# Cross attention and expert layer on one core: a new order of the attention matmuls, full-size output projection, a column scalar for spreading k, and an unrolled last loop

## The chip, the core and the metric

The kernel runs on one core of a Trainium2 chip. The metric is the time of one execution in microseconds (us), lower is better; the median of several executions is given. The core has a matrix engine (PE, TensorE), a vector engine (DVE), an activation engine (ACT), a general-purpose engine (POOL) and a queue engine that issues transfers (SP). Each engine works through its own list of instructions in order and waits on semaphores for the others.

## What is computed

128 batches of 64 tokens, 128 features, 16 heads of 8 features; float32 throughout, with causal masking and a mixture of experts after it (8 experts, two of them for each batch).

```python
x = x + xattn(layernorm(x), ctx, ctx, Wq, Wk, Wv, Wo)
x = x + ffn(layernorm(x), W1, b1, W2, b2, Wr, br, gamma, beta)
# xattn: q, k, v in 16 heads of 8
scores = einsum('bhqd,bhkd->bhqk', q, k) * 8 ** -0.5       # masked where key > query
out = einsum('bhqk,bhkd->bhqd', softmax(scores), v) @ Wo.T
# ffn: one routing decision for each batch, from the mean of its tokens
rw = softmax(x.mean(axis=1) @ Wr + br)                     # top 2 of 8, softmaxed again
h = gelu(x @ W1[e] + b1[e]); expert_out = h @ W2[e] + b2[e]
y = sum of the two weighted expert_out + x
out = (y - mean) / sqrt(var + 1e-5) * gamma + beta
```

## The kernel before

**Attention** (about 20 to 365 us) works on one batch in a *step*. Four steps make a *pair* P (its four batches share two tiles of 128 tokens and one load of the context); two pairs make one round of the loop in `steps(i)`. A step is called by its place in the pair, s0, s1, s2 or s3; a unit U is one batch. Every engine has its own `steps` with the same count, so the order within an engine is written out by hand.

- PE, in each step: two matmuls that put the causal mask into a score bank (L346, bfloat16, 128x128 array), four score matmuls on small tiles of the array (`scores`, L350, 32 rows by 64 columns), four transposes of the softmax of three steps before (`turn`, L361, whole array), four matmuls of it with v (`attend`, L374, 128 rows by 32 columns), for the unit of four steps before. Then, by step: s0 transposes and projects the next pair (L322, L323: `prep_xk`) and does an output projection (`project`, L387, tiles of 128 by 64); s1 transposes the second layer norm's result (L397) and computes q (L327, `prep_q`); s2 does an output projection (L387); s3 computes v (L334).
- Every float32 matmul that is no transpose leaves two records in the trace, so that four score matmuls are "x8".
- DVE: maximum of the scores (L769), sum of the previous unit's exponentials (L772), scores less their maximum (`scores_shifted`, L779), the reciprocal of the sum (L785), and the statistics of both layer norms.
- ACT: the exponential (`probs`, L586), the copy of the transposed softmax out of PSUM (`probsT`, L595), and by step: s0 four copies of v (L535) ahead of the exponential, then the second layer norm (L568); s1 the copy of x-transposed and k (L545), then attnT (L606) and z (L574); s2 the copy of q (L551); s3 the first layer norm (L559) and attnT.
- POOL: multiplies the exponentials by the reciprocals (L1064), and spreads k (L1032, `spread_k`): for each batch a copy of k for each of four heads, zero outside the head's rows, by a product of two broadcast tensors, two of them in s1 and two in s2. It also computes the reciprocal standard deviations (L1010 to L1015), and in s3 splits z into a high part (a cast, L1043) and the rest (L1045).

The score banks are two, used in turn; mask and scores of a unit wait until DVE has shifted the unit two before (`v_sub`). `turn` waits for POOL's product (`g_norm`), q for the copy of x-transposed (`a_xk`), the scores of s0 for the spread k (`g_km`).

**Routing** (about 365 to 391 us) is a chain of small operations on DVE with a few matmuls between: top two experts, the count of each, a list of slots in blocks of eight batches (`SLOTS` entries, 328), at least one block an expert.

**Expert layers** (about 391 to 590 us): 36 blocks in loops whose bounds are read at run time, each with split high and low products of both layers.

**The last stage** (about 595 us to the end) normalizes 16 groups of four tiles: PE centres (L523), ACT squares and takes the square root (L697, L701) in a run-time loop of four rounds of four groups, DVE takes the reciprocal (L941), scales (L945) and adds x to two of the four tiles (L953), POOL adds x to the other two (L1141), SP sends 256 KB to memory.

## Time and profile before

| | |
|---|---|
| median of 3 executions | 637.44 us (635.75 to 637.48) |
| the profiled execution | 637.03 us, its span 635.2 us |
| PE busy, share of the span | 578.2 us, 91% |
| DVE busy | 526.4 us, 83% |
| ACT busy | 498.8 us, 79% |
| POOL busy | 459.6 us, 72% |
| score matmuls, transposes, matmuls with v | 1024, 512 and 1024 records |

The profile is of one execution. A row of a timeline gives the start, the length, the engine, the line, what is written from what, and in brackets the idle time ahead with the engine whose work ended it. Matmuls overlap in the array, so their starts, and not their lengths, tell how fast they follow each other.

### The profile page before, as it was taken

The numbers are of one execution on the slowest core, as the hardware profiler recorded it, in microseconds if no ns is written. First come the engines' busy times: TensorE is split into PE (matmuls) and PEld (weight loads), VectorE is DVE, ScalarE is ACT, GpSimd is POOL, SyncE is SP. The second block draws the span as 40 slices with busy tenths as digits, with TensorE's granted clock in tenths as the row PEclk, the third lists the DMA queues.
The fourth block names the chain that finished last, engine by engine and source line by source line (L and its number), as shares of the span: only waits on it lengthen the run. The fifth ranks groups of instructions, "written<-read, shape, count | busy, mean of one in ns | idle before, by whom it ended". The sixth has DMA issues, their size and how long they took to land.

```text
span 635.2 us, 19482 instructions
## 1 busy us (share of the span) xinstructions
PE 578.2 (91%) x4737; PEld 380.8 (60%) x4737; DVE 526.4 (83%) x1473; ACT 498.8 (79%) x1131; POOL 459.6 (72%) x815
## 2 busy tenths in 40 slices
PE   4899999999999999999999726999999999999762
PEld 2455555555555555555555414787888788887652
DVE  3889898988989898989898756888888888897576
ACT  3587888888887878787888627888888898887595
POOL 5788999999999999999989654656655555564233
PEclk9999999999999999999999958999999999999787
DMA  3010100010010101010020011122312332322034
GB/s 101 27 35 11 35 25 23 18 33 25 10 32 25 33 8 33 25 33 8 17 74 2 2 34 53 52 80 79 95 58 61 89 92 61 93 62 63 21 118 147
DMA packets 55583, 30.03 MB, mean 47 GB/s; under 512 B 4856, under 2 KB 54528, under 8 KB 55552
## 3 DMA queue, kind: packets, MB, share of 16 engines
q1 hardware_dynamic: 55120, 29.47, 15.8%
q8 instruction: 13, 0.21, 0.1%
q10 hardware_dynamic: 432, 0.20, 0.1%
q14 instruction: 18, 0.15, 0.1%
HBM read 13.00 MB, written 4.19 MB: 27 GB/s over the span
## 4 chain that ended last, share of the span: by engine, by line
PE 83%; ACT 6%; issue 4%; DVE 3%; POOL 2%; ACTq 1%; DVEq 1%; DMA 0%; POOLq 0%
PE scores_banks L350 12%; PE bank_pair L361 12%; PE bank_pair L374 7%; PE bank L387 6%; PE scores_banks L346 6%; PE scores_banks L479 5%; PE scores_banks L480 5%; PE scores_banks L481 5%; PE bank_pair L492 5%; PE bank_pair L493 5%; PE bank_pair L494 5%; PE bank L334 3%; PE bank L323 2%; ACT squares L697 2%; PE bank L327 2%
## 5 line engine op out<-in xcount | busy, mean ns | idle before, releaser
L1064 POOL TENSOR_TENSOR probs<-probs,row_sum_recip 128x512 f32<-128x512 f32 x128 | 133.6, 1044 | 19.7 <-DVE row_sum_recip L785 17.7
L586 ACT ACTIVATE probs<-scores_shifted 128x512 f32<-128x512 f32 x128 | 80.8, 632 | 52.1 <-DVE scores_shifted L779 50.7
L676 ACT ACTIVATE gelu<-scores_banks,b_expert 128x512 f32<-128x512 f32 x144 | 98.6, 691 | 26.6 <-PE scores_banks L481 19.7
L1113 POOL CAST gathered<-z_hi_lo (+1 forms) x114 | 45.9, 438 | 88.8 <-PE scores_banks L481 79.2
L769 DVE TENSOR_REDUCE row_max<-scores_banks 128x8 f32<-128x512 f32 x128 | 87.5, 684 | 24.3 <-PE scores_banks L350 24.1
L772 DVE TENSOR_REDUCE row_sum<-probs 128x8 f32<-128x512 f32 x128 | 87.1, 680 | 17.2 <-ACT probs L586 17.1
L895 DVE SCALAR_TENSOR_TENSOR zT_then_yT<-bank_pair,slot_weight,zT_then_yT x288 | 74.8, 283 | 17.2 <-issue 15.8
L595 ACT ACTIVATE probsT<-bank_pair 128x512 f32<-128x512 f32 x128 | 76.2, 595 | 14.5 <-PE bank_pair L361 13.5
L779 DVE TENSOR_TENSOR scores_shifted<-scores_banks,row_max 128x512 f32<-128x512 f32 x128 | 86.9, 679 | 0.0
L361 PE MATMUL bank_pair<-ident,probs 128*128 128x128 f32 x512 | 83.9, 286 | 2.0 <-POOL probs L1064 1.6
L350 PE MATMUL scores_banks<-k_by_head,qT 32*64 32x256 f32 x1024 | 85.5, 403 | 0.0
L361 PEld LDWEIGHTS bank_pair<-ident,probs 128*128 128x128 f32 x512 | 53.6, 140 | 51.0 <-issue 41.2
L1032 POOL TENSOR_TENSOR k_by_head<-xnT_and_kT,mask_j 128x256 f32<-128x256 f32 x128 | 75.9, 614 | 4.8 <-ACT xnT_and_kT L545 4.8
L886 DVE TENSOR_TENSOR gelu_lo<-gelu,gelu_hi 128x512 fp32r<-128x512 f32 x108 | 71.3, 697 | 5.4 <-ACT gelu_hi L680 2.5
L680 ACT ACTIVATE gelu_hi<-scores_banks,b_expert 128x512 fp32r<-128x512 f32 x108 | 74.6, 691 | 0.0
L479 PE MATMUL scores_banks<-gathered,w_hi 128*128 (+1 forms) x144 | 56.5, 393 | 3.0 <-ACTq L665 1.7
L492 PE MATMUL bank_pair<-gelu_hi,w_hi 128*128 128x512 f32 x144 | 56.5, 392 | 1.2 <-DVE gelu_lo L886 1.1
L481 PE MATMUL scores_banks<-gathered,w_hi 128*128 (+1 forms) x144 | 56.1, 389 | 0.0
L494 PE MATMUL bank_pair<-gelu_lo,w_hi 128*128 128x512 f32 x144 | 56.1, 389 | 0.0
L493 PE MATMUL bank_pair<-gelu_hi,w_lo 128*128 128x512 f32 x144 | 56.1, 389 | 0.0
L480 PE MATMUL scores_banks<-gathered,w_lo 128*128 (+1 forms) x144 | 56.0, 389 | 0.0
L374 PE MATMUL bank_pair<-probsT,v_blocks 128*32 128x128 f32 x1024 | 54.5, 285 | 0.0
(169 smaller groups left out, 1168.7 us busy)
## 6 DMA issues: line engine op xcount, KB each, us to landing
gathered<-z_hi_lo SPq DMA_DIRECT2D x187, 64.0 KB, 1.8
x_res<-in_x SPq DMA_DIRECT2D x16, 256.0 KB, 2.6
ctxT_pair<-in_ctxT SPq DMA_DIRECT2D x32, 128.0 KB, 2.0
w_raw<-in_w SPq DMA_DIRECT2D x16, 256.0 KB, 3.0
out<-gelu SPq DMA_DIRECT2D x16, 256.0 KB, 2.2
gathered<-z_hi_lo ACTq DMA_DIRECT2D x3, 64.0 KB, 1.9
wq<-in_wq SPq DMA_DIRECT2D x1, 64.0 KB, 2.3
wk<-in_wk SPq DMA_DIRECT2D x1, 64.0 KB, 2.1
```

Of the source, the lines that this page charges most:

```text
L350: mm = nc.tensor.matmul(ps[64 * (r % 2):64 * (r % 2) + 64, r // 2, :], QT[rows, par, s, :], KM[rows, par, s, :, :].rearrange("p a k -> p ( ...
L361: mm = nc.tensor.transpose(T_ps[:, 128 * b:128 * b + 128], PP[:, k % 4, 128 * b:128 * b + 128], ident[:, :])
L374: mm = nc.tensor.matmul(A_ps[32 * b:32 * b + 32, 128 * (k % 2):128 * (k % 2) + 128], VM[:, par, s, 2 * b:2 * b + 2, :, :].rearrange("p a b ...
L479: nc.tensor.matmul(ps, W1H[:, par, cols], hi, start=True, stop=False)
L480: nc.tensor.matmul(ps, W1L[:, par, cols], hi, start=False, stop=False)
L481: nc.tensor.matmul(ps, W1H[:, par, cols], lo, start=False, stop=True).then_inc(p_h, 1)
L492: nc.tensor.matmul(ps, W2H[:, par, cols], GH[:, c, :], start=(c == 0), stop=False)
L493: nc.tensor.matmul(ps, W2L[:, par, cols], GH[:, c, :], start=False, stop=False)
L494: nc.tensor.matmul(ps, W2H[:, par, cols], GL[:, c, :], start=False, stop=(c == FC - 1)).then_inc(p_l2, 1)
L676: nc.scalar.activation(G[:, c, :], bank[c][:, :], ACT.Gelu, bias=b1e).then_inc(a_g if c == 0 else a_gp, 1)
L769: nc.vector.reduce_max(mx, ps, AX.X).then_inc(v_max, 1)
L1064: nc.gpsimd.tensor_tensor(pp, pp, RC[:, k % 2, :].unsqueeze(2).to_broadcast([128, 8, S]), ALU.mult).then_inc(g_norm, 1)
```

## The change

- `scores`, `attend` and `turn` stand in this order on PE in each step, instead of `scores`, `turn`, `attend`. The mask is a function of its own, for the next unit, at the end of the step; in the list of PE this is where it stood before, ahead of the scores, but the scores' waits for q and k now come after it.
- The output projection is two matmuls on the whole array instead of four on tiles of 64 columns; ACT's copy of attnT writes the two batches side by side for it.
- `spread_k` runs over heads instead of batches: each instruction multiplies k of four batches (128x256) by one column of the head mask, a tensor and a scalar for each partition.
- The high part of z is written by ACT in s2 (`keep_z_hi`), and POOL's split in s3 only subtracts.
- At least two blocks an expert; the list of slots has 368 entries instead of 328. The router's counts in these inputs give every expert two or more blocks already, so there are 36 blocks in both kernels.
- ACT's last loop is written out (four rounds in a row, no branch). In the last stage DVE adds x to one tile of a group, POOL to three. One addition of beta moves ahead of POOL's loop, and SP, ACT and DVE wait for POOL's last clearing of memory (`g_const` 6) before they use gathered batches.

```diff
-MAXBLK = (2 * NB + (GB - 1) * E) // GB
+MAXBLK = max(min((2 * NB + (GB - 1) * (E - few)) // GB, (E - few) * NB // GB) + 2 * few for few in range(E - 1))
...
+            def mask(i, k):
+
+                ge(pe, v_sub, 8 * i + k - 1)
+                for rp in range(2):
+                    nc.tensor.matmul(S_ps[k % 2][:, rp, :], identb[:, :], cmask[:, :, :].rearrange("p a k -> p (a k)"),
+                                     start=True, stop=False, skip_group_check=True)
...
                 if s == 0:
                     ge(pe, a_q, P + 1)
                     ge(pe, g_km, P + 1)
-                ge(pe, v_sub, U - 1)
-                for rp in range(2):
-                    nc.tensor.matmul(ps[:, rp, :], identb[:, :], cmask[:, :, :].rearrange("p a k -> p (a k)"),
-                                     start=True, stop=False, skip_group_check=True)
...
-                for b in range(2):
-                    for r2 in range(2):
-                        mm = nc.tensor.matmul(J1[64 * b:64 * b + 64, 0:D], AT[:, t, b, 64 * r2:64 * r2 + 64],
-                                              WOZ[:, r2, :], start=(r2 == 0), stop=(r2 == 1))
+                for r2 in range(2):
+                    mm = nc.tensor.matmul(J1[:, 0:D], AT[:, t, r2, :], WOZ[:, r2, :], start=(r2 == 0), stop=(r2 == 1))
...
                         scores(i, u)
+                    if not static or 0 <= U - 4 < NB:
+                        attend(i, u - 4)
                     if not static or 0 <= U - 3 < NB:
                         turn(i, u - 3)
-                    if not static or 0 <= U - 4 < NB:
-                        attend(i, u - 4)
...
+                    if not static or U + 1 < NB:
+                        mask(i, u + 1)
...
+            def keep_z_hi(P):
+
+                act.wait_ge(a_zt, P + 1)
+                nc.scalar.activation(Z2[:, bass.ds(4 * P, 4), 0, :],
+                                     YT[:, bass.ds(256 * P, 256)].rearrange("p (b q) -> p b q", q=S),
+                                     ACT.Copy).then_inc(a_zh, 1)
...
+                    if s == 2 and (not static or 0 <= P - 3 < NP):
+                        keep_z_hi(P - 3)
...
-            with act.Fori(0, 4) as o:
+            for o in range(4):
                 for k in range(4):
                     act.wait_ge(p_y, 4 * o + (k + 1))
...
-                nc.vector.tensor_tensor(YN[:, k, 0:2, :], YN[:, k, 0:2, :], X[:, bass.ds(16 * o + 4 * c, 2), :],
+                nc.vector.tensor_tensor(YN[:, k, 0:1, :], YN[:, k, 0:1, :], X[:, bass.ds(16 * o + 4 * c, 1), :],
...
-                for b in batches:
-                    ins = nc.gpsimd.tensor_tensor(KM[:, par, b, :, :],
-                                                  XK[:, 256 + S * b:256 + S * b + S].unsqueeze(1)
-                                                  .to_broadcast([128, 4, S]),
-                                                  jmask[:, :].unsqueeze(2).to_broadcast([128, 4, S]), ALU.mult)
-                    ins.then_inc(g_km if b == 3 else g_kmb, 1)
+                pool.nop().then_inc(g_kmb, 1)
+                for j in heads:
+                    ins = nc.gpsimd.tensor_scalar(KM[:, par, :, j, :],
+                                                  XK[:, 256:512].rearrange("p (b k) -> p b k", k=S),
+                                                  jmask[:, j:j + 1], None, ALU.mult)
+                    ins.then_inc(g_km if j == 3 else g_kmb, 1)
...
-                nc.gpsimd.tensor_copy(hi, z).then_inc(g_zh, 1)
-                pool.wait_ge(g_zh, P + 1)
+                pool.wait_ge(a_zh, P + 1)
                 nc.gpsimd.tensor_tensor(lo, z, hi, ALU.subtract).then_inc(g_zl, 1)
...
-                yn = YN[:, c % 4, 2:4, :]
+                yn = YN[:, c % 4, 1:4, :]
```

The list of PE in the loop over rounds, from the scores of a step s2 to the v projection of s3, before (L350 is the scores, L361 the transposes, L374 the matmuls with v, L387 the output projection, L346 the mask, L334 v):

```order
L350 MATMUL scores_banks<-k_by_head,qT 64x256 x4
L361 MATMUL bank_pair<-ident,probs 128x128 x4
L49 REGISTER_ALU
L374 MATMUL bank_pair<-probsT,v_blocks 32x128 x4
L387 MATMUL bank<-wo_half,attnT 64x128 x4
L49 REGISTER_ALU
L346 MATMUL scores_banks<-causal_mask,ident_bf 128x256 x2
L350 MATMUL scores_banks<-k_by_head,qT 64x256 x4
L361 MATMUL bank_pair<-ident,probs 128x128 x4
L374 MATMUL bank_pair<-probsT,v_blocks 32x128 x4
L334 MATMUL bank<-wv,ctxT_pair 128x128 x2
```

The same stretch of PE now (L354 the scores, L378 with v, L365 the transposes, L390 the projection, L343 the mask, L335 v):

```order
L354 MATMUL scores_banks<-k_by_head,qT 64x256 x4
L49 REGISTER_ALU
L378 MATMUL bank_pair<-probsT,v_blocks 32x128 x4
L365 MATMUL bank_pair<-ident,probs 128x128 x4
L390 MATMUL bank<-wo_half,attnT 128x128 x2
L49 REGISTER_ALU
L343 MATMUL scores_banks<-causal_mask,ident_bf 128x256 x2
L354 MATMUL scores_banks<-k_by_head,qT 64x256 x4
L378 MATMUL bank_pair<-probsT,v_blocks 32x128 x4
L365 MATMUL bank_pair<-ident,probs 128x128 x4
L335 MATMUL bank<-wv,ctxT_pair 128x128 x2
```

The matmuls with v and the transposes have changed places, and from the transposes to the mask all matmuls now use the whole array.

The list of ACT in the last stage before: one round of the run-time loop, with the loads of ACT's function tables that the build puts into it.

```order
L693 UNCONDITIONAL_BRANCH
L693 ISA
L697 ACT_TABLE_LOAD
L697 ACTIVATE squares,ln_var<-scores_banks 128x128 x4
L701 ACT_TABLE_LOAD
L701 ACTIVATE ln_std<-ln_var,eps 128x4
L695 REGISTER_ALU
L697 ACTIVATE squares,ln_var<-scores_banks 128x128 x4
L701 ACTIVATE ln_std<-ln_var,eps 128x4
```

And now, the start of the sixteen groups in a row:

```order
L706 COMPARE_AND_BRANCH
L714 ACTIVATE squares,ln_var<-scores_banks 128x128 x4
L718 ACT_TABLE_LOAD
L718 ACTIVATE ln_std<-ln_var,eps 128x4
L714 ACTIVATE squares,ln_var<-scores_banks 128x128 x4
L718 ACTIVATE ln_std<-ln_var,eps 128x4
```

Two loads stood in each of the four rounds; in the whole stage one load is left.

## Rows read from the trace of the kernel before

**Rows 1.** Busy time by engine in 100 to 300 us (us, instructions).
```profile
core 0: us, PE busy (x) PEld busy (x) DVE busy (x) ACT busy (x) POOL busy (x), PEclk, DMA share, GB/s
100.00:300.00 200.00, 198.39 (x2142) 110.29 (x2144) 179.09 (x501) 163.83 (x388) 182.45 (x331) 1.00 0.08 24
```

**Rows 2.** Timeline of PE, narrow windows: start, length, records still in flight.
```profile
201.96 0.33 PE L361 MATMUL bank_pair<-ident,probs 128*128 128x128 f32 x1
...
202.12 0.49 PE L361 MATMUL bank_pair<-ident,probs 128*128 128x128 f32 x3
...
202.23 0.38 PE L361 MATMUL bank_pair<-ident,probs 128*128 128x128 f32 x2
202.55 0.30 PE L374 MATMUL bank_pair<-probsT,v_blocks 128*32 128x128 f32 x1
```

**Rows 3.** Timeline of PE from q in s1 to the scores of s3.
```profile
211.28 0.60 PE L327 MATMUL bank<-xnT_and_kT,wq 128*128 128x256 f32 x2
...
212.03 0.66 PE L350 MATMUL scores_banks<-k_by_head,qT 32*64 32x256 f32 x8
212.62 0.66 PE L361 MATMUL bank_pair<-ident,probs 128*128 128x128 f32 x4
213.21 0.42 PE L374 MATMUL bank_pair<-probsT,v_blocks 128*32 128x128 f32 x8
213.56 0.67 PE L387 MATMUL bank<-wo_half,attnT 128*64 128x128 f32 x8
214.16 0.39 PE L346 MATMUL scores_banks<-causal_mask,ident_bf 128*128 128x256 bf16 x2
214.48 0.66 PE L350 MATMUL scores_banks<-k_by_head,qT 32*64 32x256 f32 x8
```

**Rows 4.** Timeline of ACT over the same pair.
```profile
207.81 0.63 ACT L586 ACTIVATE probs<-scores_shifted 128x512 f32<-128x512 f32 x1
208.47 0.60 ACT L595 ACTIVATE probsT<-bank_pair 128x512 f32<-128x512 f32 x1
...
209.87 0.63 ACT L586 ACTIVATE probs<-scores_shifted 128x512 f32<-128x512 f32 x1
210.41 0.58 ACT L545 ACTIVATE xnT_and_kT<-bank 128x512 f32<-128x512 f32 x1
...
215.76 0.60 ACT L595 ACTIVATE probsT<-bank_pair 128x512 f32<-128x512 f32 x1 [0.24 <-PE bank_pair L361]
...
218.47 0.63 ACT L586 ACTIVATE probs<-scores_shifted 128x512 f32<-128x512 f32 x1
```

**Rows 5.** Timeline of DVE at the first step of that pair.
```profile
208.47 0.69 DVE L772 TENSOR_REDUCE row_sum<-probs 128x8 f32<-128x512 f32 x1 [0.72 <-ACT probs L586]
209.08 0.68 DVE L779 TENSOR_TENSOR scores_shifted<-scores_banks,row_max 128x512 f32<-128x512 f32 x1
```

**Rows 6.** Groups by line, 100 to 300 us: count, busy, mean ns, idle ahead.
```profile
L1032 POOL TENSOR_TENSOR k_by_head<-xnT_and_kT,mask_j 128x256 f32<-128x256 f32 x74 | 43.9, 615 | 0.0
...
L574 ACT ACTIVATE zT_then_yT<-bank 128x256 f32 x19 | 7.4, 391 | 0.0
...
L1043 POOL CAST z_hi_lo<-zT_then_yT x19 | 7.5, 397 | 0.0
```

**Rows 7.** Groups by line, routing stage, DVE.
```profile
L866 DVE TENSOR_TENSOR probs<-probs 128x328 f32<-128x328 f32 x1 | 0.5, 501 | 0.0
```

**Rows 8.** Timeline of the last stage, ACT and DVE.
```profile
614.69 1.28 ACT L701 ACT_TABLE_LOAD   x1
615.99 0.30 ACT L701 ACTIVATE ln_std<-ln_var,eps 128x4 f32<-128x4 f32 x1
617.35 0.30 ACT L701 ACTIVATE ln_std<-ln_var,eps 128x4 f32<-128x4 f32 x1
...
616.32 0.18 DVE L941 RECIPROCAL ln_rstd<-ln_std 128x4 f32<-128x4 f32 x1 [1.46 <-ACT ln_std L701]
...
617.64 0.42 DVE L953 TENSOR_TENSOR gelu<-gelu,x_res 128x256 f32<-128x256 f32 x1
617.97 0.18 DVE L941 RECIPROCAL ln_rstd<-ln_std 128x4 f32<-128x4 f32 x1
...
624.46 0.18 DVE L941 RECIPROCAL ln_rstd<-ln_std 128x4 f32<-128x4 f32 x1 [1.45 <-ACT ln_std L701]
```

More of the change, by code:

```diff
@@ L283, in _ @@
             sp.wait_ge(g_zl, NP)
+            sp.wait_ge(g_const, 6)
             b = slot_batches(mybir.EngineType.SP, 0, ACG, SPG - ACG)
@@ L433, in _ @@
             pe.wait_ge(v_setup, 4)
+            mask(0, 0)
             steps(0)
@@ L605, in steps @@
                         ge(act, p_w, 4 * i + (u // 2 - 3))
-                        nc.scalar.activation(AT[:, t, :, :].rearrange("p b q -> p (b q)"),
-                                             A_ps[:, 0:256], ACT.Copy).then_inc(a_at, 1)
+                        nc.scalar.activation(AT[:, t, :, :].rearrange("p a (b q) -> p b a q", b=2),
+                                             A_ps[:, 0:256].rearrange("p (b a q) -> p b a q", b=2, a=2),
+                                             ACT.Copy).then_inc(a_at, 1)
                     if s == 1 and (not static or 0 <= P - 3 < NP):
@@ L628, in _ @@
             keep_z(NP - 1)
+            keep_z_hi(NP - 1)
             def split_hi(loads, par):
@@ L918, in _ @@
             dve.wait_ge(v_r, 7)
+            dve.wait_ge(g_const, 6)
             dve.wait_ge(v_st, 1)
@@ L1118, in _ @@
             gather(1, slot_batches(mybir.EngineType.Pool, 1, SPG, GB - SPG))
-            blocks = pool.value_load(STI[0:1, E:E + 1], min_val=1, max_val=MAXBLK)
+            blocks = pool.value_load(STI[0:1, E:E + 1], min_val=2 * NB // GB, max_val=MAXBLK)
             pool.wait_ge(a_b2, 1)
@@ L1130, in assist @@
                 nc.gpsimd.tensor_tensor(GL[:, 3, :], G[:, 3, :], GH[:, 3, :], ALU.subtract).then_inc(g_gl, 1)
-            with pool.Fori(0, NP) as g:
+            x_plus_beta(NP - 1)
+            with pool.Fori(0, NP - 1) as g:
                 assist(g)
                 x_plus_beta(g)
-            with pool.Fori(NP, blocks) as g:
+            with pool.Fori(NP - 1, blocks) as g:
                 assist(g)
             def add_x(o, c):
-                yn = YN[:, c % 4, 2:4, :]
+                yn = YN[:, c % 4, 1:4, :]
                 pool.wait_ge(v_sc, 4 * o + (c + 1))
-                nc.gpsimd.tensor_tensor(yn, yn, X[:, bass.ds(16 * o + (4 * c + 2), 2), :], ALU.add).then_inc(g_out, 1)
+                nc.gpsimd.tensor_tensor(yn, yn, X[:, bass.ds(16 * o + (4 * c + 1), 3), :], ALU.add).then_inc(g_out, 1)
             with pool.Fori(0, 4) as o:
```

9 lines of the change are left out of this document (5 added, 4 removed).

## The prediction

> **What bounds the kernel now.** I read the busy times by stage first, then the timeline of one pair of the attention loop on PE, ACT and DVE together, then the groups of POOL, then the last stage. The attention loop holds more than half of the time, and there PE is busy in 198.39 of 200 us [rows 1]. The reader is to see that this alone does not settle it. L1032 occurs 74 times in 200 us, four times a pair [rows 6], so a pair lasts 200 / 18.5 = 10.81 us; of that PE is busy 10.72, POOL 9.86, DVE 9.68, ACT 8.86 [rows 1]. Four engines stand within 2 us of each other. So what PE gives back is worth only what the next limit leaves, and the next limit is looked for as a loop through several engines, not as one engine's sum.
>
> **Part 1: PE's switches between tile sizes.** Four transposes follow each other at 201.96, 202.12, 202.23 and, by the same spacing, 202.34; the matmul with v, on tiles of another size, starts at 202.55 [rows 2]. Inside one tile size the spacing is 0.11; the first after a switch takes 0.05 more and the last before one 0.10 more. A stretch of one tile size thus costs 0.15 us on top of its records: 4 x 0.11 + 0.15 = 0.59, which is what the transposes take (212.62 to 213.21 [rows 3]). Before, a step has four stretches (mask, scores, transposes, v) and the two projections on 64 columns add two in s0 and one in s2: 19 a pair. After it has three (scores, v, whole array): 12 a pair. The projection itself is 0.60 now, 213.56 to 214.16 [rows 3], and four whole-array records are 4 x 0.11 = 0.44: the difference is the switch already counted. PE's work falls by 7 x 0.15 = 1.05, from 10.72 to 9.67 a pair.
>
> **Part 2: what the pair can fall to.** The pair has a loop that goes through ACT, DVE and PE, and it closes in the pair that the rows show. From the exponential of s3 at 207.81 to that of s3 a pair later at 218.47 [rows 4]:
> - exponential to exponential of s0: 207.81 to 209.87, 2.06. DVE needs almost the same: the sum waited 0.72 for ACT and starts at 208.47, the shift ends at 209.08 + 0.68 = 209.76 [rows 5]. So 1.98 to 2.06 stays.
> - copy of x-transposed and k: starts 0.54 later, takes 0.58, ends at 210.99 [rows 4].
> - PE's q matmul starts at 211.28 [rows 3], 0.29 after that. The hand-over alone is between 0.11 (shift's end to exponential [rows 4, 5]) and 0.29; I take 0.15. So PE has only some 0.14 of slack here: **q cannot come earlier than its copy**, however fast PE is.
> - q to the scores of s2: 211.28 to 212.03, 0.75. Unchanged.
> - scores of s2 to scores of s3: 212.03 to 214.48, 2.45 [rows 3]. After: scores 0.59, v 0.35 (213.21 to 213.56), transposes, projection and mask (4 + 4 + 2) x 0.11 + 0.15 = 1.25; 2.19 together.
> - scores of s3 to ACT's copy of the transposes: 214.48 to 215.76, 1.28 [rows 3, 4]. After, the matmuls with v stand in between: 1.28 + 0.35 = 1.63. ACT waited 0.24 for these transposes [rows 4].
> - from that copy through layer norm, attnT and four copies of v to the next exponential: 215.76 to 218.47, 2.71.
>
> The sum before is 2.06 + 0.54 + 0.58 + 0.29 + 0.75 + 2.45 + 1.28 + 2.71 = 10.66, this pair's own length; the other pair of the round is longer, which gives the mean of 10.81. After it is 2.06 + 0.54 + 0.58 + 0.15 + 0.75 + 2.19 + 1.63 + 2.71 = 10.61, or 10.53 with 1.98 for the first term. **The new order puts 0.35 us of v ahead of the transposes that ACT waits for**, and that eats what the fewer switches of this stretch give. I take 10.58: 0.23 less a pair. Thirty pairs run in this state: 7 us. In the last pairs, where POOL's products are awaited by PE, its lost cast of 0.40 and the shorter projections give some 0.7; an estimate, between 0 and 1.5.
>
> The other parts of the attention are hidden under that loop. **POOL:** the cast of z (0.40 [rows 6]) leaves, 9.46 remain. The column scalar has no row; it reads one tensor instead of two, like the cast of the same 256 elements at 0.40, and replaces the two-tensor product at 0.61 [rows 6]. Below the cast it can hardly go; above 0.61 it may, if the scalar or the strided output is dear. I take 0.40, which gives 8.6 a pair; at 0.61 it is 9.46, and both are below 10.58. It is worth nothing by itself, but it makes room: the products for the transposes come earlier, and the mean loses the excess of the longer pair. **ACT:** the high part costs what z's copy costs, 0.39 [rows 6], in s2, after the copy of the transposes, where ACT otherwise waits for DVE; 8.86 + 0.39 = 9.25 a pair. The next exponential on ACT stands behind it. If its cover is gone it costs up to 0.39 a pair. The waits of the split move from POOL to ACT's work of a step before, which is over by then. The scores' wait for k behind the mask instead of ahead of it lets the mask run; nothing to gain beyond 0.1. ACT's permuted copy of attnT has the same 256 columns: nothing, at most 0.1 on the last leg.
>
> **Part 3: the last stage.** A square root follows the other at 1.36 us (615.99, 617.35), and one round of four groups takes 624.46 - 616.32 = 8.14 on DVE, which waits 1.46 at its start for ACT's square root [rows 8]. Four groups at 1.36 are 5.44; two table loads a round make the other 2.70 (one of them at 614.69, 1.28). All but the first load of the stage's square roots go. Then DVE is late next: it takes 617.97 - 616.32 = 1.65 a group, with 0.33 from the start of its addition of 256 elements to the next reciprocal [rows 8]. The addition halves; its 128 elements fewer are worth, by the 0.42 for 256, between 0.10 and 0.21, taken as 0.13. DVE's group is then 1.52. A round falls from 8.14 to 6.08. Three rounds fall whole, 3 x 2.06 = 6.2, and the last by its shorter additions, 0.4; the first group has nothing ahead of it in both. Sum 6.6. POOL's part grows from 256 to 384 elements, which by its 0.61 for 256 is about 1.0 and below 1.52. If transfers or POOL hold the groups at 1.65, 5 us remain.
>
> **Part 4: the rest.** Routing: 40 more slots on a DVE operation of 0.50 for 328 elements [rows 7] are 0.05, about seven such on the chain and their matmuls: +0.4. Two blocks an expert change no count here. The waits for POOL's clearing of memory, which stands ahead of POOL's own weight split, and the moved addition of beta lie beside the routing chain: 0, at most +0.5.
>
> **Sum:** 637.03 - 7.0 - 0.7 - 6.6 + 0.4 = 623.1 for the profiled execution. The median of the runs shown lies 0.4 above that execution, so 623.5.
>
> **The rivals.**
> - *The loop of part 2 does not close that way* (25%): with PE ahead, DVE or ACT runs tighter than the pair shown, and the pair falls to what DVE needs, 9.68 and a part of its 0.72 wait [rows 1, 5], about 10.2. For it: DVE has that slack. Against it: the copy of x-transposed hangs on DVE's own shift. 0.6 x 30 = 18 us instead of 7: 612.
> - *PE was the bound alone* (2%): then the whole 1.05 comes back, 31 us, and the time is 599. DVE's 9.68 and its wait speak against it. The Trainium skill, page "TensorEngine Tiling", section "Tiling Modes", Key Properties, says that changing the tiling mode drains the engine; the 0.15 of rows 2 agrees, and by that rule alone, taken as the price of the change, 599 would be the forecast.
> - *The attention gives nothing* (13%): the transposes that come 0.35 later hold ACT, or the high part of z holds the exponential, and a pair stays at 10.81. Then 637.03 - 6.6 + 0.4 + 0.4 = 631.2.
> - *Slower* (5%): the column scalar on POOL is dear. POOL's 9.86 - 0.40 and about 0.5 of hand-overs between its dependent instructions make 9.96 + 4 x (t - 0.61) a pair. The rest of the change gives 6.9 us, so a pair of 11.04 makes it even: t = 0.88 us. At 1.0 the pair is 11.5 and the time 637 + 21 - 7 = 651. The 0.40 of the cast speaks against it.
> - *The unrolled loop gives little* (5%): DVE or the transfers then take 2 us a group as now: 630.
>
> **How the numbers follow.** My forecast has 50%: 623.5, with 620 to 627 from the bounds of the hand-over (0.14 x 30 = 4) and of the last stage (1.6). The range holds the first rival's 612 and the third's 631: 611.5 to 631.5; outside are the PE rival, the slower one and a little of the tails. Faster by over 0.3% (1.9 us, about what a measurement of this kernel can tell from no change) are all but the slower one and a part of small mishaps: 93%; within 3%; slower 4%.
>
> **What would show it.** A pair of 10.5 to 10.6 us between exponentials of s3; PE idle ahead of the q matmul, released by the copy of x-transposed, some 0.5 to 0.9 a pair, and PE's busy share of 100 to 300 us down to some 92%; the stretch from v to the end of mask without a gap; DVE still waiting for the exponential at s0; the column scalar near 0.40; one table load in the last stage and a cadence of 1.52 there, with DVE busy throughout. It is wrong if PE's idle time stands elsewhere (at the mask, behind DVE's shift), if the pair is below 10.4 or above 10.7, or if POOL's spread takes over 0.88.

## The result: slower by 0.9%, where 2.2% faster was forecast

| | before | after |
|---|---|---|
| median of the runs, us | 637.16 (635.05 to 637.48, 5 runs) | 642.61 (640.67 to 642.83, 5 runs) |
| span of the profiled execution, us | 635.2 | 641.1 |
| start to the first exponential of s3 | 24.08 | 26.04 |
| from there to the last exponential | 332.73 | 343.30 |
| first reciprocal of the last stage to the end | 35.1 | 28.2 |

The ratio is 1.009, with a 95% interval of 1.0066 to 1.0113. The forecast was 623.5 and the range ended at 631.5. The rival that I had given 5% is what happened: the column scalar on POOL is dear.

The last stage is 6.9 us shorter and the stretch between attention and last stage 0.3 longer. The attention stage is 12.5 us longer: 2.0 ahead of the first exponential of s3, and 10.6 in the 31 distances between exponentials of s3 that follow. From the sixth on, 24 of these are longer by 0.36 us on the mean, 8.5 together; this is where to look. The third, 13.12 us, is longer by 2.2, and its wait of the scores for k (1.87 us) does not tell why, since another of 1.83 stands ahead of the first pair, which is not longer. After this wait PE's granted clock falls to 0.50, its lower level, from 48 to 51 us, while it is 1.00 at that place in the kernel before. Such a dip also stands in experiment 7, without the column scalar: 0.50 from 26 to 29 us, and the first pair takes 12.15 us instead of 10.64. What brings it on, no run shows. The other distances nearly cancel. The busy times of 100 to 300 us, which answer [rows 1]:

```profile
core 0: us, PE busy (x) PEld busy (x) DVE busy (x) ACT busy (x) POOL busy (x), PEclk, DMA share, GB/s
100.00:300.00 200.00, 173.72 (x1935) 112.02 (x1934) 173.12 (x485) 166.10 (x394) 194.18 (x306) 1.00 0.08 24
```

PE fell from 198.39 to 173.72; the pairs are longer now, so this is to be read by the pair, and there it is 10.74 before and 9.72 now: PE's part of the change works. POOL rose from 182.45 to 194.18. The groups of POOL in this window, which answer [rows 6] (count, busy us, mean ns, idle time ahead):

```profile
L1081 POOL TENSOR_TENSOR probs<-probs,row_sum_recip 128x512 f32<-128x512 f32 x72 | 75.4, 1047 | 0.0
L1051 POOL TENSOR_SCALAR k_by_head<-xnT_and_kT,mask_j 128x256 f32<-128x256 f32 x72 | 66.1, 931 | 0.0
L1031 POOL TENSOR_TENSOR ln_rstd<-ln_rstd,minus_half 128x2 f32<-128x2 f32 x36 | 26.0, 723 | 3.0
...
L1033 POOL TENSOR_TENSOR ln_shift<-ln_shift,ln_rstd 128x2 f32<-128x2 f32 x36 | 7.1, 196 | 2.8
```

The column scalar takes 931 ns where the two-tensor product took 615 [rows 6]; I had put 400. And no large instruction of POOL has any idle time ahead of it: the only gaps are those between the small dependent steps of the layer norm, 3.0 + 2.8 us. A pair of tiles lasts 11.19 us now (mean of the distances between exponentials of s3), so the window holds 17.87 pairs: 194.18 / 17.87 = 10.87 of work and 5.8 / 17.87 = 0.32 of gaps make 11.19. **POOL is full**, and the pair is POOL's own sum. The waits of the window (total us, times, longest) show who pays:

```profile
PE scores_banks L354 <- POOL k_by_head L1051: 26.3, 18, 1.5
...
DVE row_max L786 <- PE scores_banks L354: 23.9, 36, 1.2
```

Once a pair, PE stands at the scores of s0 for the last spread of k. On the timeline the mask is through at 213.74 and the scores wait 1.47 us:

```profile
213.61 1.83 POOL L1051 TENSOR_SCALAR k_by_head<-xnT_and_kT,mask_j 128x256 f32<-128x256 f32 x2
```
```profile
213.74 0.38 PE L343 MATMUL scores_banks<-causal_mask,ident_bf 128*128 128x256 bf16 x2
215.59 0.66 PE L354 MATMUL scores_banks<-k_by_head,qT 32*64 32x256 f32 x8 [1.47 <-POOL k_by_head L1051]
```

The second spread ends at 213.61 + 1.83 = 215.44, the scores start 0.15 after. The page tells the same from the other side: the chain that ended last has POOL as its largest part, by its products and its spreads. Before, PE alone had 83% of it and POOL 2%.

```profile
POOL 37%; PE 33%; issue 16%; DVE 6%; ACT 3%; POOLq 2%; ACTq 1%; DVEq 1%; DMA 0%
POOL probs L1081 12%; POOL k_by_head L1051 10%; POOL ln_rstd L1031 6%; PE scores_banks L484 5%; PE bank_pair L497 5%; PE scores_banks L486 5%; PE scores_banks L485 5%; PE bank_pair L499 5%; PE bank_pair L498 5%; POOL z_hi_lo L1062 3%; DVE gelu L963 2%; POOL ln_shift L1029 2%; POOL ln_rstd L1028 1%; POOL ln_shift L1033 1%; PE scores_banks L354 1%
```

The last stage did what was forecast. It has one table load (before: two in each of the four rounds, as the list of ACT shows), and DVE's groups follow each other at 617.27 - 615.75 = 1.52 us:

```profile
611.21 1.28 ACT L718 ACT_TABLE_LOAD   x1
```
```profile
615.75 0.17 DVE L959 RECIPROCAL ln_rstd<-ln_std 128x4 f32<-128x4 f32 x1
617.27 0.17 DVE L959 RECIPROCAL ln_rstd<-ln_std 128x4 f32<-128x4 f32 x1
```

### The profile page after: what moved, and what is told of

Its sections match the earlier page's. It is cut to its first block, busy times and chain, and to the rows that moved or that the text cites. A ratio compares the mean times of both kernels' runs of the same rounds, so it can differ in the third digit from the quotient of the medians.

```text
span 641.1 us, 19009 instructions
## 1 busy us (share of the span) xinstructions
PE 546.3 (85%) x4481; PEld 387.9 (61%) x4481; DVE 524.0 (82%) x1473; ACT 502.3 (78%) x1156; POOL 494.5 (77%) x783
## 4 chain that ended last, share of the span: by engine, by line
POOL 37%; PE 33%; issue 16%; DVE 6%; ACT 3%; POOLq 2%; ACTq 1%; DVEq 1%; DMA 0%
POOL probs L1081 12%; POOL k_by_head L1051 10%; POOL ln_rstd L1031 6%; PE scores_banks L484 5%; PE bank_pair L497 5%; PE scores_banks L486 5%; PE scores_banks L485 5%; PE bank_pair L499 5%; PE bank_pair L498 5%; POOL z_hi_lo L1062 3%; DVE gelu L963 2%; POOL ln_shift L1029 2%; POOL ln_rstd L1028 1%; POOL ln_shift L1033 1%; PE scores_banks L354 1%
## 5 line engine op out<-in xcount | busy, mean ns | idle before, releaser
L354 PE MATMUL scores_banks<-k_by_head,qT 32*64 32x256 f32 x1024 | 85.6, 403 | 44.5 <-POOL k_by_head L1051 44.4
L1051 POOL TENSOR_SCALAR k_by_head<-xnT_and_kT,mask_j 128x256 f32<-128x256 f32 x128 | 117.5, 931 | 5.4 <-issue 3.4
L365 PE MATMUL bank_pair<-ident,probs 128*128 128x128 f32 x512 | 84.4, 288 | 0.2
L354 PEld LDWEIGHTS scores_banks<-k_by_head,qT 32*64 32x64 f32 x1024 | 27.6, 131 | 73.4 <-issue 73.4
L365 PEld LDWEIGHTS bank_pair<-ident,probs 128*128 128x128 f32 x512 | 53.8, 141 | 25.9 <-issue 18.5
L378 PE MATMUL bank_pair<-probsT,v_blocks 128*32 128x128 f32 x1024 | 54.5, 285 | 2.2 <-ACT attnT L620 1.8
```

Source lines behind the costliest of these rows:

```text
L354: mm = nc.tensor.matmul(ps[64 * (r % 2):64 * (r % 2) + 64, r // 2, :], QT[rows, par, s, :], KM[rows, par, s, :, :].rearrange("p a k -> p ( ...
L365: mm = nc.tensor.transpose(T_ps[:, 128 * b:128 * b + 128], PP[:, k % 4, 128 * b:128 * b + 128], ident[:, :])
L1051: ins = nc.gpsimd.tensor_scalar(KM[:, par, :, j, :], XK[:, 256:512].rearrange("p (b k) -> p b k", k=S), jmask[:, j:j + 1], None, ALU.mult)
```

## The experiments

"Pair" is always the mean distance between exponentials of s3 in the steady part of the attention stage. The kernel before has 10.83, the changed one 11.19.

**1. The column scalar out, the rest of the change kept.** POOL spreads k by batch with the two-tensor product, as the kernel before does.

```
-                pool.nop().then_inc(g_kmb, 1)
-                for j in heads:
-                    ins = nc.gpsimd.tensor_scalar(KM[:, par, :, j, :],
-                                                  XK[:, 256:512].rearrange("p (b k) -> p b k", k=S),
-                                                  jmask[:, j:j + 1], None, ALU.mult)
+                for b in heads:
+                    ins = nc.gpsimd.tensor_tensor(KM[:, par, b, :, :],
+                                                  XK[:, 256 + S * b:256 + S * b + S].unsqueeze(1)
+                                                  .to_broadcast([128, 4, S]),
+                                                  jmask[:, :].unsqueeze(2).to_broadcast([128, 4, S]), ALU.mult)
...
```

> The changed kernel with one part undone: POOL spreads k by batch with a product of two broadcast tensors, as before. Theory: the column scalar alone (0.93 us where 0.61 stood) made the attention longer; without it a pair falls from 11.19 us to the 10.58 that the prediction worked out, PE waits ahead of the q matmul for the copy of x-transposed, and the kernel takes 623 to 625 us. Rival 1: the new order and ACT's high part cost something of their own; then a pair is 10.8 or more and the kernel takes 630 us or more. Rival 2: the loop through ACT, DVE and PE does not bind; then a pair is about 10.2 and the kernel takes 612 us.

Measured: 626.47 us (624.87 to 627.38, 4 runs), ratio to before 0.982 (0.980 to 0.985); pair 10.70. The window 100 to 300 and its largest waits:

```profile
100.00:300.00 200.00, 186.67 (x2023) 117.13 (x2022) 179.78 (x506) 169.12 (x410) 178.22 (x317) 1.00 0.08 24
```
```profile
DVE row_sum L789 <- ACT probs L598: 18.3, 19, 1.0
...
POOL probs L1081 <- DVE row_sum_recip L802: 13.3, 19, 0.7
ACT probsT L607 <- PE bank_pair L365: 6.3, 18, 0.4
PE scores_banks L354 <- POOL k_by_head L1050: 5.4, 18, 0.3
PE bank L399 <- DVE x_res L750: 5.1, 19, 0.3
```

POOL waits again, for DVE, and the wait of the scores for k falls from 26.3 to 5.4. So this one instruction cost 642.61 - 626.47 = 16.1 us and turned a gain into a loss. What is left of the error, 626.5 against 623.5, is mainly the pair: it gives 0.13 (10.83 to 10.70) where the forecast had 0.23 less, which is 3.0 us over 30 pairs. Smaller differences at the start (1.4 later than before) and between attention and last stage (0.9 shorter, forecast 0.4 longer) cancel.

**2. Is it the layout or the operation?** The spread goes by head as in the change, with its strided output, but as a product of two tensors.

```
-                    ins = nc.gpsimd.tensor_scalar(KM[:, par, :, j, :],
-                                                  XK[:, 256:512].rearrange("p (b k) -> p b k", k=S),
-                                                  jmask[:, j:j + 1], None, ALU.mult)
+                    ins = nc.gpsimd.tensor_tensor(KM[:, par, :, j, :],
+                                                  XK[:, 256:512].rearrange("p (b k) -> p b k", k=S),
+                                                  jmask[:, j:j + 1].unsqueeze(2).to_broadcast([128, 4, S]), ALU.mult)
```

> The changed kernel, k still spread by head (four batches of one head, 128x256, the output in four strided pieces), but as a product of two tensors, the head's column broadcast over the 256 elements. If the layout by head is what costs, the instruction stays at 0.9 us and a pair at 11.2. If the column scalar is what costs, the instruction takes 0.61 us as the one by batch did, and a pair and the whole time are those of the run with the spreading by batch.

Measured: 625.61 us in one run, instruction 0.613 us, pair 10.70. The layout is innocent. (One run; the reading rests on the instruction and the pair.)

**3. and 4. Is it the column operand or the scalar form, and what has one input?** Both leave out the zeros between heads, so the scores and with them the routing are others. Only the instruction and the pair of these runs can be read, and not their times (one run each, 626.26 us with the constant and 618.91 with the copy).

```
                     ins = nc.gpsimd.tensor_scalar(KM[:, par, :, j, :],
                                                   XK[:, 256:512].rearrange("p (b k) -> p b k", k=S),
-                                                  jmask[:, j:j + 1], None, ALU.mult)
+                                                  1.0, None, ALU.mult)
```

> The changed kernel with its spread of k by head multiplied by the constant 1.0 instead of the column of the mask: the zeros between heads are left out, so the scores are others and the routing with them; only the instruction and the length of a pair are to be read. If it is the column operand that costs, the instruction falls from 0.93 to about 0.40 us, as the cast has; if it is the form with a scalar at all, it stays at 0.93 and the pair at 11.19.

```
-                    ins = nc.gpsimd.tensor_scalar(KM[:, par, :, j, :],
-                                                  XK[:, 256:512].rearrange("p (b k) -> p b k", k=S),
-                                                  jmask[:, j:j + 1], None, ALU.mult)
+                    ins = nc.gpsimd.tensor_copy(KM[:, par, :, j, :],
+                                                XK[:, 256:512].rearrange("p (b k) -> p b k", k=S))
```

> The changed kernel with its spread of k by head made by a plain copy: the zeros between heads are left out here too, and only the instruction and the length of a pair are to be read. A copy of 128x256 took 0.397 us in the kernel before; with this layout I expect 0.40 to 0.45 us, and a pair of at most 10.70 us. If writing by head is dear in a form with one input, it takes over 0.6.

The group of the spread in the one and in the other:

```profile
L1051 POOL TENSOR_SCALAR k_by_head<-xnT_and_kT 128x256 f32<-128x256 f32 x74 | 62.0, 853 | 0.0
```
```profile
L1051 POOL COPY k_by_head<-xnT_and_kT 128x256 f32<-128x256 f32 x76 | 28.0, 399 | 4.1 <-ACT xnT_and_kT L550 2.6 <-issue 1.5
```

With a constant it still takes 0.853 us, with a plain copy 0.399. So it is neither the column (0.08 of it) nor reading one tensor, but the scalar operation itself: 0.45 more than the copy of the same elements to the same places. Of the two outcomes named ahead for the constant, 0.40 and 0.93, neither came. VectorE working beside POOL is no explanation either: all 128 column spreads of the changed kernel take 925 to 943 ns, and the seven that have VectorE idle for more than half of their length take 932 on the mean. Why the scalar operation takes so long on POOL, no run shows. With three prices for one place in the program, and the fourth from the change, there is a curve:

| spread, us | 0.399 | 0.614 | 0.853 | 0.931 |
|---|---|---|---|---|
| pair, us | 10.70 | 10.70 | 10.83 | 11.19 |
| POOL's busy time of 200 us | 162.67 | 178.22 | 194.01 | 194.18 |
| POOL's sum a pair, gaps of 0.32 included | 9.0 | 9.86 | 10.83 | 11.19 |

Up to 0.614 the pair does not feel POOL; at 0.853 and 0.931 it equals POOL's sum. From 9.86 + 4 (t - 0.614) = 10.70 the two meet at t = 0.82 us, an estimate that lies between the measured points.

**5. The column scalar alone.** The kernel before, with nothing but its spread changed to the column scalar by head.

```
-                    ins = nc.gpsimd.tensor_tensor(KM[:, par, b, :, :],
...
+                    ins = nc.gpsimd.tensor_scalar(KM[:, par, :, j, :],
+                                                  XK[:, 256:512].rearrange("p (b k) -> p b k", k=S),
+                                                  jmask[:, j:j + 1], None, ALU.mult)
...
```

> The kernel before with one part of the change alone: k spread by head with the column scalar. Theory: POOL becomes the bound: its pair is 9.86 us busy before, 0.5 of hand-overs, and 4 x 0.32 more, 11.6 us; thirty pairs at 0.8 more and about 2 us at the start make 637 + 26 = 663 us. Rival: the column scalar is only dear beside the new order of PE and ACT; then it takes 0.61 here or less and the time stays within 2 us of 637.

Measured: 665.12 us (664.48 to 666.78, 4 runs), ratio 1.043 (1.041 to 1.046); instruction 0.927, pair 11.74. POOL is full here too: 191.30 us of work in 200 / 11.74 = 17.04 pairs are 11.23, the gaps of the layer norm are 0.32, and a gap of 0.19 stands between the cast of z and the subtraction that needs it (3.2 us in 17 waits); together 11.74. The same edit costs 28 us by itself and 16 in company of the others, because there the cast (0.40) and its gap (0.19) have left POOL: its full pair is 11.19 instead of 11.74, and the pair without the column, 10.70 instead of 10.83, gives back 0.13 of that.

**6. What TensorE's part is worth.** Everything of experiment 1, but TensorE as before: the masks directly ahead of their scores, transposes ahead of the matmuls with v, the projection in halves, and ACT's copy of attnT as that projection needs it.

```
-                for r2 in range(2):
-                    mm = nc.tensor.matmul(J1[:, 0:D], AT[:, t, r2, :], WOZ[:, r2, :], start=(r2 == 0), stop=(r2 == 1))
+                for b in range(2):
+                    for r2 in range(2):
+                        mm = nc.tensor.matmul(J1[64 * b:64 * b + 64, 0:D], AT[:, t, b, 64 * r2:64 * r2 + 64],
+                                              WOZ[:, r2, :], start=(r2 == 0), stop=(r2 == 1))
...
                 if s == 0:
                     ge(pe, a_q, P + 1)
                     ge(pe, g_km, P + 1)
+                mask(i, k)
...
-                    if not static or U + 1 < NB:
-                        mask(i, u + 1)
```

> The kernel before with everything of the change but TensorE's part: z's high part on ACT, the last loop written out, two or more blocks an expert, the two-tensor product by batch kept, and TensorE's mask, scores, transposes, attend and the projection in halves as before. If TensorE's part is what shortened the attention stage, the pair is the old 10.83 us and the time is that of before less the last stage: 637.5 - 6.9 + 0.3 = 631. The rival, that leaving POOL's cast out did it, gives 10.70 and 627.

Measured: 631.62 us (630.67 to 632.23, 4 runs), ratio 0.991 (0.988 to 0.993); pair 10.82, as in the kernel before (10.83). Against experiment 1 the medians differ by 5.1 us. Of the 4.8 between the two profiled executions, 4.0 lie between the first exponential of s3 and the last one, and these are TensorE's part; 0.9 come from a single late group in the last stage (2.36 us instead of 1.52). ACT's high part and POOL's freed 0.4 us do nothing for the pair.

**7. The last loop alone.** The kernel before with `for o in range(4):` in place of `with act.Fori(0, 4) as o:` in ScalarE's last loop.

> The kernel before with one edit: ScalarE's last loop is written out (four rounds instead of a loop of four). If the table loads of that loop were what set the last stage, it is bound by VectorE's group next, at 1.65 us a group as its rows in the kernel before have it: 3 rounds of 8.14 become 3 of 6.60, less 4.6, and the first and last round some 1 more, so 632. The rival, that the loop on ScalarE was not the bound and the split of the last addition is what moved the stage, gives under 1 us: 637.

Measured: 633.01 us (631.60 to 633.88, 4 runs), ratio 0.993 (0.991 to 0.995). One table load is left, and DVE's groups are 1.65 us apart, as the forecast read them from [rows 8]:

```profile
603.20 0.17 DVE L941 RECIPROCAL ln_rstd<-ln_std 128x4 f32<-128x4 f32 x1
604.85 0.17 DVE L941 RECIPROCAL ln_rstd<-ln_std 128x4 f32<-128x4 f32 x1
```

From the first reciprocal to the end it is 30.2 us, against 35.1 before and 28.2 with the whole change: the loop gives 4.9 (4.1 by the medians), the new split of the addition 2.0.

**8. Transposes back ahead of the matmuls with v.** The forecast had found that the new order puts v's 0.35 us ahead of the transposes for which ACT waits. Experiment 1 with that one exchange:

```
-                    if not static or 0 <= U - 4 < NB:
-                        attend(i, u - 4)
                     if not static or 0 <= U - 3 < NB:
                         turn(i, u - 3)
+                    if not static or 0 <= U - 4 < NB:
+                        attend(i, u - 4)
```

> The run with the spreading by batch, and PE's transposes put back ahead of the matmuls with v; mask at the end, full-size projection, ACT's high part and the unrolled last loop stay. If the loop through ACT, DVE and PE binds as the prediction worked out, its sum with this order is 2.06 + 0.54 + 0.58 + 0.15 + 0.75 + 2.34 + 1.28 + 2.71 = 10.41 us a pair, though PE has four more switches of tile size (4 x 0.15 = 0.6 us more work a pair): faster than the run with the new order by 0.15 to 0.2 us a pair, 5 us in all. If PE's own work binds, it is slower than that run, by up to 0.6 us a pair, 18 us.

Measured: 624.49 us (622.99 to 625.36, 4 runs), ratio 0.979 (0.977 to 0.982); pair 10.61. PE has four more switches of tile size a pair and is busy 196.38 of 200 us instead of 186.67, and the kernel is faster by 2. The steps of one pair, on ACT and on PE, first of experiment 1:

```profile
206.94 0.63 ACT L598 ACTIVATE probs<-scores_shifted 128x512 f32<-128x512 f32 x1
...
209.00 0.63 ACT L598 ACTIVATE probs<-scores_shifted 128x512 f32<-128x512 f32 x1
209.54 0.58 ACT L550 ACTIVATE xnT_and_kT<-bank 128x512 f32<-128x512 f32 x1
...
215.00 0.60 ACT L607 ACTIVATE probsT<-bank_pair 128x512 f32<-128x512 f32 x1 [0.34 <-PE bank_pair L365]
```
```profile
217.70 0.63 ACT L598 ACTIVATE probs<-scores_shifted 128x512 f32<-128x512 f32 x1
```
```profile
211.16 0.66 PE L354 MATMUL scores_banks<-k_by_head,qT 32*64 32x256 f32 x8
...
213.36 0.66 PE L354 MATMUL scores_banks<-k_by_head,qT 32*64 32x256 f32 x8
```

and with the transposes first:

```profile
204.38 0.63 ACT L598 ACTIVATE probs<-scores_shifted 128x512 f32<-128x512 f32 x1
...
206.44 0.63 ACT L598 ACTIVATE probs<-scores_shifted 128x512 f32<-128x512 f32 x1
206.98 0.58 ACT L550 ACTIVATE xnT_and_kT<-bank 128x512 f32<-128x512 f32 x1
```
```profile
212.28 0.60 ACT L607 ACTIVATE probsT<-bank_pair 128x512 f32<-128x512 f32 x1 [0.19 <-PE bank_pair L365]
...
214.97 0.63 ACT L598 ACTIVATE probs<-scores_shifted 128x512 f32<-128x512 f32 x1
```
```profile
208.60 0.66 PE L354 MATMUL scores_banks<-k_by_head,qT 32*64 32x256 f32 x8
...
210.99 0.66 PE L354 MATMUL scores_banks<-k_by_head,qT 32*64 32x256 f32 x8
```

Laid beside the forecast's own terms they are:

| term | forecast | experiment 1 | transposes first |
|---|---|---|---|
| exponential of s3 to that of s0 | 2.06 | 2.06 | 2.06 |
| to the copy, and the copy | 0.54 + 0.58 | 0.54 + 0.58 | 0.54 + 0.58 |
| copy's end to the scores of s2 | 0.15 + 0.75 | 1.04 | 1.04 |
| scores of s2 to scores of s3 | 2.19 | 2.20 | 2.39 |
| to ACT's copy of the transposes | 1.63 | 1.64 | 1.29 |
| to the next exponential of s3 | 2.71 | 2.70 | 2.69 |
| sum | 10.61 | 10.76 | 10.59 |

The transposes reach ACT 0.35 us sooner, the one switch put back between these scores costs 0.19 (0.15 by the forecast's price), and 0.17 is left in this pair, 0.09 in the mean of the two kinds of pair. The direction was right and the 0.35 was right; the switch takes half of it back. The size was not: 10.41 a pair and 5 us were expected, 10.61 and 2 us came. And the table finds the forecast's one wrong term: from the copy to the scores it was to be 0.90, and is 1.04, as it was before the change.

Beside the table stands something that the forecast did not work out. Pairs of two kinds take turns in the kernel before, 10.66 and 11.01 us, and the forecast's terms are of the shorter kind. In experiment 1 that kind is longer, 10.76: it saves 0.25 between the scores, loses 0.36 ahead of ACT's copy, and its q comes no sooner. The whole gain lies in the other kind, which falls from 11.01 to 10.65. Its copy of x-transposed and its q, before and in experiment 1:

```profile
220.99 0.58 ACT L545 ACTIVATE xnT_and_kT<-bank 128x512 f32<-128x512 f32 x1
222.29 0.60 PE L327 MATMUL bank<-xnT_and_kT,wq 128*128 128x256 f32 x2
```
```profile
220.22 0.58 ACT L550 ACTIVATE xnT_and_kT<-bank 128x512 f32<-128x512 f32 x1
221.06 0.60 PE L328 MATMUL bank<-xnT_and_kT,wq 128*128 128x256 f32 x2
```

Before, q stood 0.72 us behind the end of the copy, since PE went without a gap from 218.76 to 222.29; now it stands 0.26 behind. So **PE's own work bound every second pair**, and only there did its saving come back.

**9. and 10. That term.** In experiment 1, PE stands in s1 at the transposes of z for DVE's residual (5.1 us in 19 waits), with q queued behind. So I let q go first.

```
+                    if s == 1 and more:
+                        prep_q(P + 1)
                     if s == 1 and (not static or 0 <= P - 3 < NP):
                         turn_z(P - 3, 4 * i + 2 * h - 2 if not static else min(2 * P - 2, NT))
-                    if s == 1 and more:
-                        prep_q(P + 1)
```

On top of experiment 1:

> The kernel of e1 (the change with the two-tensor product by batch), with one edit: in slot 1 TensorE forms q before it transposes z. In e1 TensorE stood at the z transpose for VectorE's residual (bank L399 <- x_res L750, 5.1 us in 19 waits of the window 100 to 300), with q queued behind it, and q is on the loop that sets a pair of tiles. If that hand-over is the missing part of my loop sum, the pair goes from 10.70 to about 10.57 us and the time from 626.5 to 622.5. The rival, that the spread of k (5.4 us of waits of the scores on k_by_head) or POOL's product sets the pair, leaves 10.70 and 626.5.

and on top of experiment 8:

> The kernel of e6 (two-tensor product, transposes ahead of attend) with the same edit as e8: q ahead of the z transpose. If both hand-overs are parts of one loop, the gains add: pair 10.61 to about 10.48 us, time 624.5 to 620.5. The rival, that with the transposes first the loop already runs through POOL's product and no longer through q, leaves 10.61 and 624.5.

Measured: 629.23 us (627.21 to 630.10) with a pair of 10.80, and 625.25 us (624.61 to 626.23) with a pair of 10.64, 4 runs each. Neither gains: the first lost 2.8 us, and in the second the difference lies within the spread. **My explanation fell.** The timelines of PE say why. Experiment 1, where ACT's copy ends at 210.12:

```profile
210.17 0.41 PE L399 MATMUL bank<-ident,z_pair 128*128 128x128 f32 x2 [0.30 <-DVE x_res L750]
210.41 0.60 PE L328 MATMUL bank<-xnT_and_kT,wq 128*128 128x256 f32 x2
210.85 0.38 PE L343 MATMUL scores_banks<-causal_mask,ident_bf 128*128 128x256 bf16 x2
211.16 0.66 PE L354 MATMUL scores_banks<-k_by_head,qT 32*64 32x256 f32 x8
```

and with q first, where the copy ends at 210.42:

```profile
210.47 0.70 PE L328 MATMUL bank<-xnT_and_kT,wq 128*128 128x256 f32 x2 [0.31 <-ACT xnT_and_kT L550]
211.00 0.38 PE L399 MATMUL bank<-ident,z_pair 128*128 128x128 f32 x2
211.22 0.38 PE L343 MATMUL scores_banks<-causal_mask,ident_bf 128*128 128x256 bf16 x2
211.53 0.66 PE L354 MATMUL scores_banks<-k_by_head,qT 32*64 32x256 f32 x8
```

From the copy's end to the scores of s2 it is 1.04 us in the first and 1.11 in the second. Both matmuls stand ahead of those scores whichever is first, and q is no shorter when it starts an idle PE: 0.53 to the next record instead of 0.44. In addition ACT now waits for the transposes of z:

```profile
ACT zT_then_yT L579 <- PE bank L399: 6.5, 19, 0.3
```

The wait for DVE's residual is there, but taking q past it wins nothing, since the transposes of z then stand between q and the scores. Whether the 0.14 would come back if they had their turn before the copy's end, with DVE's residual earlier or with a bank of their own, was not tried and stays open.

**11. The high part of z.** Experiment 8 with the cast back on POOL.

```
-                    if s == 2 and (not static or 0 <= P - 3 < NP):
-                        keep_z_hi(P - 3)
...
+                nc.gpsimd.tensor_copy(hi, z).then_inc(a_zh, 1)
                 pool.wait_ge(a_zh, P + 1)
```

> The kernel of e6 with the cast of z's high part back on POOL (0.40 us a pair there, against 0.41 on ACT). My prediction gave moving it no time of its own, since it lay beside other work on either engine: then the pair stays within 0.05 of 10.61 us and the time within 2 of 624.5, with POOL busy some 185 of 200 us in the middle window. The rival: POOL is so full that 0.40 more delays its product and the spread; half of it on the path gives 0.2 more a pair, 630.5.

Measured: 623.75 us (623.53 to 624.17, 4 runs), ratio 0.979 (0.977 to 0.981); pair 10.62. It can't be told from the 624.49 of experiment 8. POOL's busy time goes from 179.04 to 186.09 and ACT's from 170.83 to 165.06, and the pair stays. With the two-tensor product, moving the cast is worth nothing. With the column scalar, where POOL is the bound, its time and its gap are POOL's own: 11.74 a pair with the cast on POOL (experiment 5, with PE as before) against 11.19 without. That pairing was not run by itself.

## Right and wrong, step by step

- **The column scalar: wrong, and the step that decides.** "It reads one tensor instead of two, like the cast of the same 256 elements at 0.40 ... I take 0.40." It takes 0.93. The paragraph itself says that it may go above 0.61, and then works out the pair for 0.40 and 0.61 alone. The operation did stand in the trace, in a small form that I had not used: L1029 (L1011 in the kernel before), POOL's multiplication of 128x2 elements by the constant -1.0. It takes 0.229 us (0.222 before), with 0.196 for the product of two tensors of that size (L1033). There too the scalar form is the dearer one, which would have been a warning, though not a price: how it grows shows only with the large form. From 2 to 256 elements the multiplication by a constant grows by (0.853 - 0.229) / 254 = 2.5 ns an element, the product by (0.614 - 0.196) / 254 = 1.6. The Trainium skill, page "GPSIMD Engine Reference", section 4.1 (Engine selection), says that on POOL operations with two inputs are about twice as slow as on VectorE and those with one input run at roughly line rate. No run here has the copy on VectorE, so that the rate itself can't be compared; but the scalar multiplication, with one tensor to read, is not priced like the copy (0.399 us): at 0.853 and 0.931 us it is slower than the two-input product at 0.614. The measurement decides.
- **The slower rival: right in mechanism and size, wrong in its chance.** Its formula 9.96 + 4 (t - 0.61) gives 11.24 at t = 0.93, against 11.19, and its break-even of t = 0.88 was passed. At 0.853 it gives 10.93, against 10.83. It had 5%. For an operation whose price was a guess, on the engine with the second highest busy time, that was too little, and the range should have reached to it.
- **Part 1, the switches of tile size: right.** Scores to scores in the changed order was put at 2.19 us. The changed kernel has 209.66 to 211.85, which is 2.19. The saving of 0.25 between these starts, in experiment 1 (2.45 to 2.20), was put at 0.26. The busy times agree less well: PE's fell by 1.02 a pair in the changed kernel and by 0.75 in experiment 1, where 1.05 was forecast.
- **Part 2, the loop: right in its terms but for one, and worked out for one kind of pair only.** With POOL's product as before the pair is 10.70, not 10.58; against the kernel before it gains 0.13 instead of 0.23, and that is 3.0 us over 30 pairs. The term is the copy's end to q, taken at 0.15 of a measured 0.29, as if the rest were slack that the faster PE takes up; the transposes of z and their wait for DVE kept it. All others came within 0.02. But the sum was made of the shorter kind of pair, and that kind did not fall: it went from 10.66 to 10.76. What the mean gained came from the longer kind (11.01 to 10.65), where q had waited 0.72 us behind its copy for PE's own work. The forecast has only "the mean loses the excess of the longer pair", and lays it to the room that POOL gets. Experiment 6, with POOL's cast gone and PE as before, keeps pairs of 10.65 and 10.98: it was PE's work, not POOL's room. So the direction was found, and that the size came near is partly luck. That PE's 1.05 us would mostly not come back, and that v ahead of the transposes eats part of it, held (experiments 1, 6 and 8).
- **The cast and ACT's high part: right.** Worth nothing each, as long as POOL is not the bound (experiment 11). In the changed kernel POOL is the bound, and by POOL's sum the move kept the loss smaller there.
- **Part 3, the last stage: right.** 6.9 us, forecast 6.6; groups at 1.52 us as forecast. Experiments 7 and the change split it into 4.9 for the loop and 2.0 for the addition, where the forecast had, by the same terms, 4.6 + 2.0.
- **Part 4, the routing: not decided.** The stretch is 0.3 us longer, forecast 0.4. But the runs that share this code with the changed kernel and its results have it between 1.3 shorter (experiment 2) and 0.3 longer (experiment 8), so that 0.4 can't be told from nothing.
- **The tell-tales.** "It is wrong if POOL's spread takes over 0.88" is what the profile shows. The wait at s0 moved from ACT and DVE to PE's scores, released by POOL. PE's idle time ahead of q, put at 0.5 to 0.9 us a pair and released by the copy, is not in experiment 1 either: there PE waits 0.3 a pair ahead of the transposes of z, for DVE.

623.5, plus 3.0 for what the loop did not give, plus 16.1 for the column scalar is 642.6. This closes by its making, since both are differences of measured times. What checks it are the pairs: 0.10 x 30 = 3.0 for the first and 0.49 x 30 = 14.7 for the second; the 1.4 that is left of the second is not taken apart.

The best of these kernels is the change with the two-tensor product and the transposes first, 624.49 us, or 623.75 with the cast left on POOL, which can't be told apart: both take 0.979 of the time of the kernel before, and 0.979 / 1.009 = 0.97 of that of the changed one.

## What to carry to other kernels

When an edit exchanges one operation for another on an engine that is over 90% busy, do not price it by one with the same count of inputs. A row of the same operation with a small operand can warn (here 0.22 us against 0.20), and only a row or a run at full size gives the price; without one, and with the break-even within reach, let the range go past it. An engine that is nearly full has a threshold: at 0.614 us this instruction was harmless, at 0.853 it was not, and at 0.931 it cost 16 us. If pairs of two lengths take turns, work out both: here the gain came from the one that was not read. In a loop through several engines, the order of what is awaited counts for more than the engine's busy time, and a wait on the path is worth only what stands free behind it.

## What the chip showed that I had not expected

On POOL, for 128x256 elements of f32, a copy took 0.399 us, a cast 0.397, the product of two tensors, one or both of them broadcast, 0.614, a multiplication by a constant 0.853 and one by a column of scalars 0.931. Even the addition of two whole tensors of that size, which POOL does in the last stage of the kernel before (L1141), took only 0.730. The scalar forms have less to read and are the dearest. I had also not expected that q, started by an idle PE, takes 0.09 us longer to the next record than one that follows other matmuls.
